# Stacking attention rows channel-major through DRAM, with seven expert units moved to later stages

## What is computed

```python
h = concat([mix(x), W_E[x_txt] * 16], axis=1)                 # 384 x 256
n = layernorm(h)
q, k, v = (n @ Wq + bq) / 4, n @ Wk + bk, n @ Wv + bv         # 16 heads of 16
w = q @ k.T + rel_to_abs(q @ emb_rel_k)                       # +-4 neighbours
p = softmax(w)
h = h + (p @ v + abs_to_rel(p) @ emb_rel_v) @ Wo + bo
n = layernorm(h); r = routing_weights(n)
h = h + sum_e r[e] * ((silu(n @ Wg[e]) * (n @ Wu[e])) @ Wd[e])
```

## Time and profile before

| | us |
|---|---|
| median of 3 runs (lowest, highest) | 1346.44 (1345.1, 1354.54) |
| the profiled execution's own time | 1361.19 |
| its span | 1359.4 |
| PE busy | 1139.8 (84%) |
| DVE busy | 750.2 (55%) |
| ACT busy | 370.3 (27%) |
| DMA queue of SP, share of 16 engines | 31.9% |

### The profile page before, as it was taken

How to read it: one execution, slowest core, us unless ns; L and a number is a source line. 1 busy time by engine, 2 the same in 40 slices (tenths; PEclk the granted TensorE clock), 3 DMA queues, 4 the chain that set the end, 5 groups by cost and what they waited for, 6 DMA issues and landing times.

```text
span 1359.4 us, 16898 instructions
## 1 busy us (share of the span) xinstructions
PE 1139.8 (84%) x5668; PEld 801.1 (59%) x5668; DVE 750.2 (55%) x1579; ACT 370.3 (27%) x599; POOL 234.3 (17%) x258
## 2 busy tenths in 40 slices
PE   5447689878898798988899788997999889898798
PEld 4311379526784377735785277852787457762587
DVE  6336363673547546484546735485454745567443
ACT  1204312062211622134120621216121351205211
POOL 5404220031200402012200412004020122003100
PEclk9667779898999988899898987998889997999989
DMA  6592207402092102901065020921119010460200
GB/s 221 145 202 77 44 5 111 107 1 60 1 168 49 36 24 54 162 1 36 24 103 114 1 59 0 164 54 29 30 48 168 2 36 24 84 133 1 47 0 12
DMA packets 126842, 89.59 MB, mean 66 GB/s; under 512 B 67847, under 2 KB 116360, under 8 KB 126378
## 3 DMA queue, kind: packets, MB, share of 16 engines
q1 hardware_dynamic: 126408, 88.05, 31.9%
q0 software_dynamic: 384, 1.05, 0.3%
HBM read 60.36 MB, written 28.71 MB: 66 GB/s over the span
## 4 chain that ended last, share of the span: by engine, by line
PE 32%; issue 26%; DVE 15%; DMA 12%; SPq 6%; ACT 5%; POOL 3%; POOLq 0%; DVEq 0%; ACTq 0%
DMA scratch<-d_band_t 9%; PE S L878 7%; PE S L754 5%; PE S L746 4%; DVE S L1187 4%; PE S L899 4%; SPq L538 4%; PE S L809 4%; ACT scratch L996 3%; PE S L710 3%; DVE maxima L1166 3%; PE S L794 2%; DMA txt_row<-in_L_txt_W_E,txt_idx 1%; PE S L627 1%; DMA w_d<-in_L_ffn_Wu 1%
## 5 line engine op out<-in xcount | busy, mean ns | idle before, releaser
L1166 DVE TENSOR_REDUCE maxima<-S 128x2 f32<-128x768 f32 x192 | 177.1, 954 | 86.7 <-PE S L754 83.9
L1434 POOL TENSOR_TENSOR bands<-scratch,one 64x432 f32<-64x432 f32 x128 | 119.7, 935 | 598.3 <-ACT scratch L996 593.2
L899 PE MATMUL S<-w_d,hT 128*128 128x256 f32 x768 | 189.4, 395 | 1.6 <-DVE hT L1308 0.7
L746 PE MATMUL S<-k_st,q_st 128*128 128x384 bf16 x384 | 140.7, 366 | 49.3 <-DMA scratch<-d_band_t 35.6
L1033 ACT ACTIVATE silu<-S 128x384 f32<-128x384 f32 x128 | 63.0, 492 | 436.2 <-PE S L878 382.1
L1187 DVE TENSOR_TENSOR S<-S,bands 64x144 f32<-64x144 f32 x384 | 154.5, 402 | 44.7 <-PE S L794 35.0
L996 ACT ACTIVATE scratch<-S 128x768 f32<-128x768 f32 x192 | 155.7, 812 | 56.6 <-DVE S L1187 49.2
L899 PEld LDWEIGHTS S<-w_d,hT 128*128 128x128 f32 x768 | 150.5, 199 | 25.0 <-issue 3.7
L754 PE MATMUL S<-scratch,ident_b 128*128 128x132 bf16 (+1 forms) x384 | 155.0, 404 | 0.0
L1308 DVE TENSOR_TENSOR hT<-silu,S 128x384 f32<-128x384 f32 x128 | 70.7, 552 | 130.5 <-PE S L878 120.7
L794 PE MATMUL S<-q_st,k_st 128*128 128x384 bf16 x384 | 94.0, 344 | 35.7 <-ACT scratch L996 34.5
(11 more groups left out here) (157 smaller groups left out, 1488.4 us busy)
## 6 DMA issues: line engine op xcount, KB each, us to landing
bands<-d_band_s SPq DMA_DIRECT2D x16, 864.0 KB, 8.7
scratch<-d_band_t SPq DMA_DIRECT2D x8, 1632.0 KB, 16.9
d_parts<-scratch SPq DMA_DIRECT2D x48, 192.0 KB, 2.0
q_st<-d_parts SPq DMA_DIRECT2D x48, 192.0 KB
k_st<-d_parts SPq DMA_DIRECT2D x48, 192.0 KB
d_band_w<-bands SPq DMA_DIRECT2D x32, 240.0 KB, 3.8
out<-scratch SPq DMA_DIRECT2D x8, 384.0 KB, 2.5
x_in<-in_x SPq DMA_DIRECT2D x8, 256.0 KB, 3.6
```

The source lines that it names most:

```text
L746: pe.matmul(S[:, bank, PAD:PAD + T], q_st[:, h, i * P:(i + 1) * P], k_st[:, h, :], start=True, stop=False, skip_group_check=True)
L899: mm = pe.matmul(D[:, i // 2, (i % 2) * E:(i % 2 + 1) * E], hT[:, (FT * e + m) % 3, i * P:(i + 1) * P], w_d[:, e, m, :], start=(m == 0), s ...
L1166: dve.tensor_reduce(dst, S[:, c0:c0 + 2, PAD:PAD + T], AX, ALU.max).then_inc(max_done.sem, 1)
L1434: nc.gpsimd.tensor_tensor(bands[rows, :, :, 2 * pair:2 * pair + 2].rearrange("p i w h -> p h i w"), win, one[rows].unsqueeze(2).unsqueeze( ...
```

## The change

q and k are now stacked channel-major. The columns of Wq and Wk are permuted on the chip once (`prepare`: loads go to `w_in`, four DVE copies write w_q and w_k), so that a projected row p = d * 8 + g holds channel d of heads 2g and 2g+1. `d_parts` keeps rows of 2 x 384, and a stack transfer reads, for each d, eight rows as one run of 12,288 bytes and writes it to partition 8d + 2 + n: 16 partitions, eight apart. Partitions 0 and 1 carry the negated maxima and the ones. Biases and `emb_k_rows` are loaded in the same order, 48 small transfers in place of 10, `head_of_row` is no longer loaded, and `rel_k` is built with a mask of eight heads. The fills change: 13 units after `project_v`, 8 in the maxima, 3 in negate, 13 in the output stage, with 48 in all as before.

```diff
@@ -46,7 +46,8 @@
 FI = 256
 FT = FI // P
 SLOTS = 6
-KST = SLOTS * AD
+G8 = P // AD
+NEG = 2
 Q_PART = [0, 0, 1, 0, 2, 1]
 K_PART = [0, 1, 0, 2, 0, 1]
 BL = 64
@@ -70,17 +71,17 @@
 EPS = 1e-5
 ITEMS = AH * TT // 2
 WINS = P // BL
-N_LOADS = (9, 4, 13 + P // AD + NJ)
+N_LOADS = (9, 4, 10 + 3 * AD + NJ)
 N_ZERO = 8
-N_CONSTS = 7
+N_CONSTS = 11
 
 FILL_MIX = [("residual", 0), ("mix_in", 0), ("turn_x2", 0), ("mix_sums", 0), ("router", 1),
             ("mix_out", 0), ("router_zone", 1), ("mix_norm", 1), ("router_rank", 2),
             ("norm_stats", 2), ("router_pick", 1), ("turn_norm", 2), ("project_qk", 0),
-            ("project_rel", 1), ("project_v", 20)]
-FILL_MAXIMA = [0, 0, 0, 1, 0, 0, 0, 1, 0, 0, 0, 1, 0, 0, 0, 1, 0, 0, 0, 1, 0, 0, 0, 0]
-FILL_NEGATE = 2
-FILL_OUT = [("turn_outputs", 3), ("turn_attn", 5), ("turn_weights", 1), ("rel_values", 1)]
+            ("project_rel", 1), ("project_v", 13)]
+FILL_MAXIMA = [0, 0, 1] * 8
+FILL_NEGATE = 3
+FILL_OUT = [("turn_outputs", 4), ("turn_attn", 6), ("turn_weights", 1), ("rel_values", 2)]
 R_DIST = 4
 ZONE_LO = float(np.float32(0.5 - np.log(4.0 / 3.0)))
 ZONE_HI = 0.5
@@ -117,7 +118,6 @@
 
         ident = sb("ident", [P, P])
         ident_b = sb("ident_b", [P, P], BF16)
-        head_of_row = sb("head_of_row", [P, KT, AH])
         head_of_rel = sb("head_of_rel", [P, AH])
         earlier = sb("earlier", [P, NE, NE])
         wkv = sb("wkv", [F + 1, 2 * F])
@@ -212,6 +212,7 @@
 
 
         emb_k_rows = zone(7640, NJ)
+        row_head, w_in = zone(7700, AH // KT), zone(6528, 2, KT, E)
         emb_v_rows, half_head = zone(7656, AD, rows=HJ), zone(7672, HH, rows=HJ)
 
         rel_log_b = Z[:, 4272:4272 + TT * RJ // 2].bitcast(BF16).rearrange("p (i r) -> p i r", i=TT)
@@ -229,7 +230,7 @@
         REL_BANKS = (O, S[:, 2])
 
 
-        d_parts = nc.dram_tensor("d_parts", [6, E, T], BF16, kind="Internal").ap()
+        d_parts = nc.dram_tensor("d_parts", [6, P, KT, T], BF16, kind="Internal").ap()
         d_zero = nc.dram_tensor("d_zero", [2, AH, T], BF16, kind="Internal").ap()
         d_neg = nc.dram_tensor("d_neg", [2, 2, AH // 2, T], BF16, kind="Internal").ap()
         d_band_t = nc.dram_tensor("d_band_t", [T * ROWB], BF16, kind="Internal").ap()
@@ -445,12 +447,10 @@
                 (ln_g[:], a["L0_tok_ln_g"].partition_broadcast(P)),
                 (ln_b[:], a["L0_tok_ln_b"].partition_broadcast(P)),
             ], [
-                (head_of_row[:], a["head_of_row"]), (head_of_rel[:], a["head_of_rel"]),
+                (head_of_rel[:], a["head_of_rel"]),
                 (earlier[:], a["earlier"]),
-                (bq4[:], a["L0_attn_bq"].rearrange("(k p) -> p k", p=P)),
-                (bk1[:], a["L0_attn_bk"].rearrange("(k p) -> p k", p=P)),
-                (w_q[:], a["L0_attn_Wq"].rearrange("(k p) n -> p k n", p=P)),
-                (w_k[:], a["L0_attn_Wk"].rearrange("(k p) n -> p k n", p=P)),
+                (w_in[:, 0], a["L0_attn_Wq"].rearrange("(k p) n -> p k n", p=P)),
+                (w_in[:, 1], a["L0_attn_Wk"].rearrange("(k p) n -> p k n", p=P)),
                 (w_v[:], a["L0_attn_Wv"].rearrange("(k p) n -> p k n", p=P)),
                 (w_o[:], a["L0_attn_Wo"].rearrange("(k p) n -> p k n", p=P)),
                 (bv_all[:], a["L0_attn_bv"].partition_broadcast(P)),
@@ -460,9 +460,12 @@
             ]]
 
             emb_v = a["L0_attn_emb_rel_v"]
-            for r in range(P // AD):
-                groups[2].append((emb_k_rows[AD * r:AD * (r + 1)],
-                                  a["L0_attn_emb_rel_k"].rearrange("o j d -> d (o j)")))
+            for d in range(AD):
+                rows = slice(d * G8, (d + 1) * G8)
+                groups[2] += [
+                    (emb_k_rows[rows], dram(a["L0_attn_emb_rel_k"], d, (0, G8), (AD, NJ))),
+                    (bq4[rows], dram(a["L0_attn_bq"], d, (KT * AD, G8), (AD, KT))),
+                    (bk1[rows], dram(a["L0_attn_bk"], d, (KT * AD, G8), (AD, KT)))]
             for j in range(NJ):
                 groups[2].append((emb_v_rows[HH * j:HH * (j + 1)], dram(emb_v, j * AD, (0, HH), (1, AD))))
 
@@ -530,14 +533,14 @@
 
                 def part_out(n, done, k, out):
                     sp.wait_ge(done.sem, done.at(b, k))
-                    sp.dma_start(d_parts[n].rearrange("(m p) t -> p m t", p=P), parts[n]
+                    sp.dma_start(d_parts[n], parts[n]
                                  ).then_inc(out.sem, 16)
 
                 def stack(st, base, order):
                     for n in range(SLOTS):
                         sp.dma_start(
-                            st[AD * n:AD * (n + 1)],
-                            d_parts[base + order[n]].rearrange("(h d) t -> d h t", d=AD)
+                            st[NEG + n:P:G8].rearrange("p h t -> p (h t)"),
+                            d_parts[base + order[n]].rearrange("(d g) m t -> d (g m t)", d=AD)
                         ).then_inc(stacked.sem, 16)
 
                 part_out(0, proj_act, 3, q_out)
@@ -556,7 +559,7 @@
                     sp.wait_ge(sc_pe.sem, sc_pe.at(b - 1, ITEMS))
                 else:
                     sp.wait_ge(pool_consts, 8)
-                sp.dma_start(q_st[KST:KST + 2], d_zero).then_inc(stacked.sem, 16)
+                sp.dma_start(q_st[0:NEG], d_zero).then_inc(stacked.sem, 16)
                 sp.wait_ge(q_out.sem, q_out.at(b, 3))
                 stack(q_st, 0, Q_PART)
                 sp.wait_ge(k_out.sem, k_out.at(b, 3))
@@ -589,7 +592,7 @@
                 sp.dma_start(d_neg[half].rearrange("i h t -> h i t"), neg_max[:]
                              ).then_inc(neg_out.sem, 16)
                 sp.wait_ge(neg_out.sem, neg_out.at(b, half + 1))
-                sp.dma_start(q_st[KST:KST + 2, half * AH // 2:(half + 1) * AH // 2], d_neg[half]
+                sp.dma_start(q_st[0:NEG, half * AH // 2:(half + 1) * AH // 2], d_neg[half]
                              ).then_inc(neg_in[half].sem, 16)
 
             def windows_back(b):
@@ -1110,10 +1113,20 @@
 
             def prepare(b):
                 dve.wait_ge(loaded[2], 16 * N_LOADS[2])
+                dve.tensor_tensor(row_head, head_of_rel[:, 0:AH // KT], head_of_rel[:, AH // KT:AH], ALU.add
+                                  ).then_inc(row_mask, 1)
+                dve.memset(rel_k[:], 0.0).then_inc(row_mask, 1)
+                dve.wait_ge(row_mask, 2)
                 for m in range(KT):
-                    dve.tensor_tensor(rel_k[:, m], emb_k_rows.unsqueeze(2).broadcast_to([P, NJ, AH]),
-                                      head_of_row[:, m].unsqueeze(1).broadcast_to([P, NJ, AH]), ALU.mult
+                    dve.tensor_tensor(rel_k[:, m].rearrange("p j (g m) -> p m j g", m=KT)[:, m],
+                                      emb_k_rows.unsqueeze(2).broadcast_to([P, NJ, AH // KT]),
+                                      row_head.unsqueeze(1).broadcast_to([P, NJ, AH // KT]), ALU.mult
                                       ).then_inc(consts, 1)
+                for n, w in enumerate((w_q, w_k)):
+                    for k in range(KT):
+                        dve.tensor_copy(w[:, k].rearrange("p (m d g) -> p m d g", m=KT, d=AD),
+                                        w_in[:, n, k].rearrange("p (g m d) -> p m d g", m=KT, d=AD)
+                                        ).then_inc(consts, 1)
                 dve.tensor_tensor(half_head, head_of_rel[0:HJ, 0:HH], head_of_rel[0:HJ, HH:AH], ALU.add
                                   ).then_inc(half_mask, 1)
                 dve.wait_ge(half_mask, 1)
@@ -1339,10 +1352,10 @@
                 nc.gpsimd.memset(dst[:], value).then_inc(pool_consts, 1)
             nc.gpsimd.memset(v_one[:], 1.0).then_inc(pool_consts, 1)
             pool.wait_ge(pool_consts, 5)
-            nc.gpsimd.memset(k_st[KST:P], 0.0).then_inc(pool_consts, 1)
-            nc.gpsimd.memset(q_st[KST:P], 0.0).then_inc(pool_consts, 1)
+            nc.gpsimd.memset(k_st[:], 0.0).then_inc(pool_consts, 1)
+            nc.gpsimd.memset(q_st[:], 0.0).then_inc(pool_consts, 1)
             pool.wait_ge(pool_consts, 7)
-            nc.gpsimd.memset(k_st[KST:KST + 2], 1.0).then_inc(pool_consts, 1)
+            nc.gpsimd.memset(k_st[0:NEG], 1.0).then_inc(pool_consts, 1)
             pool.wait_ge(pool_consts, 8)
 
             def root(b, stats, steps, done, tiles):
```

More of the change, by code:

```diff
@@ L249, in fusion_block @@
         temp_inverse, wr_high, consts = sem("temp_inverse"), sem("wr_high"), sem("consts")
+        row_mask = sem("row_mask")
         half_mask = sem("half_mask")
```

## The result

The changed kernel is slower: 1385.14 us (median of 4 runs, 1383.0 to 1387.27) against 1350.49 for the kernel before on the same chip (1345.1 to 1361.05), a ratio of 1.0278 (95% interval 1.0222 to 1.0334). The forecast was 1343, with 1364 as the upper end. Its profiled execution took 1383.0 us (span 1381.2, mean granted clock 0.897). Executions of the kernel before lie anywhere from 1337 to 1367 us, by how many stretches of PE ran at half clock; the four of the changed one differ by 4 us. The mean granted clock goes with it: 0.919 in an execution of 1337.8 us, 0.896 in the profiled one of 1361.19.

The account below looks back on a forecast made before the run. Bound: the DMA queue of stacks and PE's fill, ending close together before the maxima. Seven rounds +3.1, clock -1.5 and round 0 -5.5 sum to -3.9 us, carried to the median 1346.44: 1343 us, range 1319 to 1364.

Parts of the forecast that it names:

- seven units: Fill behind project_v, 20 units to 13: the moved units are worth 8.57 us and cost 9.55 downstream per round.
- stacks too slow: Rival, start of the maxima: the transfer sets it; decided at 200 GB/s, 1360 us; at 160 GB/s 1384; chance 0.15.
- g: Stack transfers: how much earlier the data come, 18.9 - 9.8 = 9.1 us.
- Negate: Negate stage, three units in place of two: attention later by +0.85 us a round.
- Output stage: Output stage, 13 units in place of 10: +4.5 us a round, with 1.4 of new wait for the hidden product.
- The periods of the maxima: Maxima with eight units in place of five: period 2.84 us + unit, stage 32.85 for 28.65, +4.2.
- at the 0.47 us of an issue: Round 0, small loads on SP: 37 more issues are 17.4 us; delay 2.2 to 6, taken 3.6.
- PE and SP follow the data by all of g: Round 0, which has no fill: the gain is all 9.1 us, net -5.5 after the delay of 3.6.
- I take 240 GB/s, between the mean and the geometric mean of the ends: Stack transfers: rate between ends of 125 and 409 GB/s, so a drain of 9.8 us.
- less the last (0.86), which lies under DVE's last maximum: End of the maxima: the last down is hidden, so units cost 8.56 us of 9.42; last period 4.05.
- The difference carries over: Baseline: -3.9 us against the profiled execution of 1361.19 also holds against the median 1346.44, giving 1343.
- Clock: Maxima of seven rounds: a shorter wait before them gives 1.5 us back in all; without any wait 9.6.

Follow-up runs that it names:

- e7: Changed kernel with 24 small loads for 48 and the fills of before (20, 5, 2 and 10 units): 1320.49 us, ratio 0.9777.
- e6: Changed kernel with 24 small loads for 48, each filling 16 partitions eight apart: 1370.87 us, ratio 1.0146.
- e4: Changed kernel with stacks written to 16 adjacent partitions, runs of 12,288 bytes kept: 1437.01 us.
- e5: Changed kernel with a stack transfer's 16 partitions two apart, long runs kept: 1386.97 us.
- e8: Changed kernel with 15 units behind project_v for 13 and six in the maxima for eight: 1358.71 us, ratio 1.0042.
- e2: Kernel before with only the fills of the change (13, 8, 3 and 13 units): 1414.5 us, ratio 1.0499.
- e9: Changed kernel with the last down of the maxima moved behind negate's transposes: 1406.34 us.
- b_again: Kernel before, unchanged, profiled once more: 1337.8 us.
- e1: Changed kernel's layout, loads and stack transfers with the fills of before (20, 5, 2 and 10 units): 1336.44 us, ratio 0.9893.
- e10: e7 with the five units of the maxima moved behind project_v, 25 there and none in the maxima: 1346.11 us, ratio 0.9969.

## Why the prediction was wrong

What was right: the mechanism and its sign in each part. The queue sets the start of the maxima once seven units are gone (the rival *stacks too slow*, decided at g = 7.1 or 200 GB/s, is close to what happened, though for its price the rival needed 160 GB/s). Negate: +0.58 for +0.85. Output stage: 21.40 - 17.04 = +4.36 for +4.5, with 1.26 of new wait at the place named for 1.4. The periods of the maxima between the first and the last: without the excess of these two, the stage is 35.76 - 2.05 - 1.18 = 32.53 for 32.85. The wrong steps, by size:

1. **Round 0, +14.6 us**, in two steps. 9.3 of it are the delay, 12.9 for 3.6: the step "at the 0.47 us of an issue". It priced 48 loads by one shape of load. The bias loads, eight partitions of two 4-byte elements, take 0.68 us each on SP, and with gaps three take 1.94. Ends of issue 47.85 for 38.8. The other 5.2 are the gain behind it, the step "PE and SP follow the data by all of g": from the projections to the attention stage are 66.5 us for 70.4, 3.9 less where the forecast had 9.1 (5.3 less in e7, with half the loads). Net +9.1 for round 0 where the forecast had -5.5. e6 takes 14.3 us back with half the loads. I called 2.2 to 6 the bounds, but the upper end rested on the same 0.47: a bound that is worked out from one unproven price is no bound.

2. **The stack rate, about 1.8 us a round, 13 in all.** The step "I take 240 GB/s, between the mean and the geometric mean of the ends". It is 219; g is 24.79 - 17.48 = 7.3 for 9.1. The rate is only 1.0 of these 1.8 us: at 219 GB/s the sum itself gives g = 8.1. The other 0.8 fits the old rate, 125 GB/s read from a window of 2 us: over 14 us the kernel before moves 133, which is 17.7 us for 18.9. The page of the Trainium skill was put beside the sum as the lesser estimate (218 GB/s, g = 8.1), and it was the better one: a mechanism with a checkable trait (64 partitions get half of 128, which the earlier trace rows show) stood against an average of two far ends. e4 and e5 show that the choice of partitions decides, and not the run or the extent.

3. **The first period of the maxima, about 2.05 us a round.** The forecast had a wait of 1.1 and a clock that gives 1.5 back in all. With 1.8 us less of g the wait is 2.76 in the mean of the rounds, and behind it the clock is at 1.2 GHz in every round: 6.62 us for 4.57 in the fifth, 6.0 to 6.8 in all. This is step 2 carried on: one too small g is paid twice, as wait and as clock. e8, whose fill meets the data, shows 1.00 at this place.

4. **The end of the maxima, 1.18 us a round.** The step "less the last (0.86), which lies under DVE's last maximum". The last down does lie there, but its accumulation does not: DVE does the last maxima, then three accumulated tiles (1.26 us), and the transposes of negate write the same bank and wait 1.36. The last period is 5.23 for 4.05. I had looked for what the *maxima* wait for, not at what comes behind the last unit. This wait did not exist before, since there the last unit before the transposes was an up, whose product no transpose waits for. That four items stood behind it is not the reason: in e8 six items stand behind the last down, and the wait is 1.44. e2 shows it with the old layout too; e9 shows that to move the last down behind the transposes costs more.

5. **The baseline, 17 us.** "The difference carries over" was no more than an assumption. The trace of before was of a long execution, 1361.19 us and 14.75 above the median of 1346.44; its surplus was mostly half-clock stretches, which vary from execution to execution (b_again: 1337.8). The profiled execution of the changed kernel lay 2.1 us below its median. A change of -3.9 us was far inside this spread.

Together: between the two profiled executions the change is +21.8 us (round 0 +9.1, the seven rounds +14.3, the last stage -1.5), where the forecast had -3.9 (-5.5, +1.6 and nothing). That is 25.7 too little, and with the baseline's 16.9 it makes the 42.6 between 1342.5 and 1385.1. The seven rounds are 12.7 of it. Steps 2 to 4 alone come to 7 (1.8 + 2.05 + 1.18 - 0.32 - 0.27 - 0.14) = 30, against stages of the kernel before at full clock; the last three terms are what the middle periods, negate and the output stage came to less than forecast. But its profiled execution had lost some 19 us of clock in its own rounds: 9.6 in the maxima (30.02 in the mean for 28.65), 4.8 from there to the attention stage (3.61 for 2.92), the rest mostly from the residual to the next projections. The term *Clock* gave 1.5 of that back. So it was too small for the execution that the sum was made against, and this hid more than half of the other errors in the rounds. That is luck, and it did not last: item 5, the step to the median, puts nearly as much back.

And one thing that the sum had, but that I did not draw the conclusion from. Its own terms said that seven units cost 9.55 downstream and that the data come 9.1 earlier, of which PE would have used 1.5 without any move (its wait): the move was a loss by its own numbers, and what was left of the gain was round 0 and the clock. The cheaper question, what the layout gives with the fills left alone, has its answer in e1: the fill of 20 units covers the queue almost wholly, so the layout frees only 1.66 us and the clock, and that is the whole gain a round has with this order of units. Where did the 7.3 us go? 1.66 would have come anyway; for the other 5.6 PE gave up 8.57 us of cover and paid 12.1 later (7.1 in the maxima, 0.6 in negate, 4.4 in the output). Seven times 12.1 - 5.6 is 45 of the 49 us between e1 and the changed kernel.

## What to carry to other kernels

Work that covers a transfer is free only where it stands now: before moving it, price the place that it goes to, including what is behind the last moved piece (its accumulation, where that stands in the other engine's order, its bank), and compare that with what the faster transfer really frees, which is the time to the *next* limit and not the transfer's own gain. A transfer that writes few partitions should have them spread; the spread need not be wide (16 of them two apart ran at 215 GB/s, eight apart at 219, adjacent at 131). Read a rate over the whole of the transfers, not over 2 us of them. Small loads are paid by the issue, and by their shape: count them, and make them few by letting each write strided partitions.

## What the runs showed of the hardware

- Sixteen partitions per transfer: adjacent 133 GB/s over 14 us (runs of 768 bytes) and 131 over 16 (runs of 12,288), two apart 215, eight apart 219; 64 adjacent 203, 128 partitions 403 to 409. Longer runs made nothing, the choice of partitions 64 to 67%.
- SP issues a stack of 12,288-byte runs every 0.62 us (six in 3.72); of a load of eight partitions by two 4-byte elements 0.68, by nine elements 0.46; of sixteen partitions eight apart 0.59 to 0.60 for either (e7).
- Waits of 2.6 to 3.1 us before the maxima were followed by 1.2 GHz in every round (after). Short ones were followed by it in some rounds and not in others: in the kernel before and b_again the stage took 29.87 behind a wait of 0.66 us and 28.63 behind one of 1.11 (28.65 at full clock). In e8, with waits of up to 0.6 us, the clock stayed up through the stage. In e10 it fell in mid-stage with PE busy 12.83 of 14 us and then 3.20 of 4 just before; with units in between (e1, 26.65 of 29) it stayed at 2.4 GHz through the stage. What in the two makes the difference was not tried.
- The same kernel (before) had profiled executions of 1361 and 1338 us; their PE busy times are 25.1 us apart with the same work.
